# A cross-attention and FFN kernel on one core: waits reordered in all stages, and the first normalisation applied on ACT

## The reference

```python
q = X @ Wq.T + bq;  k = ctx @ Wk.T + bk;  v = ctx @ Wv.T + bv
scores = einsum('bgrqd,bgkd->bgrqk', q, k) / sqrt(16)   # masked, causal if given
out = softmax(scores) @ v;  x = x + out @ Wo.T + bo
# FFN on layernorm(x): bitlinear158 = rms_norm, 8-bit activations, ternary weights
h = layer_norm(gelu(silu(bitlinear158(x, w1, b1))), ln_g, ln_b)   # 2048 wide
x = x + bitlinear158(h, w2, b2)
```

## Time and profile before

| | us |
|---|---|
| median of 3 runs | 621.9 |
| lowest, highest | 619.96, 622.6 |
| the profiled execution | 622.59 |
| its span in the trace | 620.8 |
| PE busy | 524.9 (85%) |
| DVE busy | 489.0 (79%) |
| ACT busy | 350.8 (57%) |
| POOL busy | 135.0 (22%) |
| mean granted clock of PE | 0.926 |

### The profile page before, as it was taken

One profiled execution on the slowest core, in us unless ns is written; L12 is line 12 of the kernel. 1 busy time (PEld: TensorE's weight loads), 2 busy tenths in 40 slices (PEclk: granted clock), 3 DMA queues, 4 the chain that ended last, 5 costly groups with the idle time before them and its releaser, 6 DMA issues.

```text
span 620.8 us, 8914 instructions
## 1 busy us (share of the span) xinstructions
PE 524.9 (85%) x3374; PEld 289.5 (47%) x3374; DVE 489.0 (79%) x728; ACT 350.8 (57%) x424; POOL 135.0 (22%) x101
## 2 busy tenths in 40 slices
PE   4778497689889999999999999999869969698446
PEld 4666133362456355645564556455425523343222
DVE  3769939349699978997899789988896887648784
ACT  0244280517584867486748674867187739287630
POOL 5030031100611061106110611301140113103220
PEclk9989598797989999999999999999969989799688
DMA  8588637934422641365136412642134221100000
GB/s 315 152 234 324 211 84 191 386 116 146 86 67 105 183 99 36 125 195 114 36 124 191 102 54 76 191 98 74 40 86 102 74 75 17 38 0 1 34 34 35
DMA packets 32994, 72.17 MB, mean 116 GB/s; under 512 B 7167, under 2 KB 14529, under 8 KB 29950
## 3 DMA queue, kind: packets, MB, share of 16 engines
q1 hardware_dynamic: 31798, 71.26, 38.8%
q10 hardware_dynamic: 1152, 0.31, 0.2%
HBM read 46.50 MB, written 20.61 MB: 108 GB/s over the span
## 4 chain that ended last, share of the span: by engine, by line
PE 58%; DVE 12%; DMA 10%; ACT 9%; issue 7%; SPq 2%; POOL 1%; ACTq 1%; DVEq 0%
PE FF L853 9%; PE FF L678 7%; PE PV L792 7%; PE FF L901 6%; ACT PT L1069 5%; PE PV L775 5%; PE S L759 5%; PE S L735 5%; DVE negm L1337 4%; PE S L888 3%; PE FF L855 2%; PE PV L735 2%; DMA work<-in_w 2%; PE FF L867 2%; DMA num<-o_raw 2%
## 5 line engine op out<-in xcount | busy, mean ns | idle before, releaser
L1069 ACT ACTIVATE PT<-S 128x1024 f32<-128x1024 f32 x128 | 123.6, 1033 | 28.1 <-PE S L759 28.0
L1337 DVE TENSOR_REDUCE negm<-S 128x4 f32<-128x1024 f32 x88 | 105.6, 1215 | 24.7 <-PE S L735 23.2
L759 PE MATMUL S<-Q,K 100*128 100x512 bf16 x256 | 78.0, 413 | 27.7 <-ACT PT L1069 18.3
L775 PE MATMUL PV<-PT,vaug 128*32 128x256 f32 x1024 | 71.8, 400 | 0.4 <-ACT PT L1069 0.4
L853 PE MATMUL FF<-w1t,xqT 128*128 128x512 bf16 x256 | 67.4, 386 | 2.0 <-ACT PT L1100 1.1
L1100 ACT ACTIVATE work<-FF,s 128x512 f32<-128x512 f32 x56 | 38.5, 687 | 40.6 <-PE FF L855 40.6
L792 PE MATMUL PV<-wo_sb,num 128*128 128x512 f32 x128 | 59.9, 614 | 0.4 <-DVE negm L1337 0.4
L678 PE MATMUL FF<-xnT,wq_sb 128*128 128x256 f32 x224 | 52.8, 394 | 8.6 <-ACT xnT L1039 8.6
L735 PE MATMUL S<-K,Q 97*128 97x256 bf16 x352 | 54.5, 282 | 6.6 <-issue 3.5
L759 PEld LDWEIGHTS S<-Q,K 100*128 100x128 bf16 x256 | 18.7, 101 | 77.4 <-ACT PT L1069 54.8
L1337 DVE TENSOR_REDUCE negm<-PV 128x4 f32<-128x1024 f32 x40 | 48.8, 1221 | 6.3 <-PE PV L735 5.9
(11 more groups left out here) (196 smaller groups left out, 858.5 us busy)
## 6 DMA issues: line engine op xcount, KB each, us to landing
Q<-q_d SPq DMA_DIRECT2D x15, 768.0 KB
work<-in_w SPq DMA_DIRECT2D x8, 1024.0 KB, 11.4
q_d<-part SPq DMA_DIRECT2D x8, 768.0 KB, 3.6
x_sb<-in_x SPq DMA_DIRECT2D x8, 512.0 KB, 4.0
ctx_sb<-in_ctxT SPq DMA_DIRECT2D x8, 512.0 KB, 4.0
q_d<-part SPq DMA_DIRECT2D x8, 512.0 KB, 3.3
xb_sb<-in_x SPq DMA_DIRECT2D x8, 512.0 KB, 3.9
rec<-rec_d SPq DMA_DIRECT2D x30, 128.0 KB, 2.6
```

What stands on the lines that cost most here:

```text
L759: last = pe.matmul(where, K[0:ROWS_2, g, kt * P:(kt + 1) * P], Q[0:ROWS_2, g, 2 * pair:2 * pair + 2, :], start=not masked, stop=True)
L775: last = pe.matmul(PV[32 * r:32 * r + 32, g % 4, :], vaug[:, c % 2, kt, g, :], PT[:, n % PT_SLOTS, r, :], start=(kt == 0), stop=(kt == TT ...
L1069: act.activation(PT[:, n % PT_SLOTS, :, :], ST[n % 2][:], ACT.Exp, scale=0.25).then_inc(S["pt_made"], 1)
L1337: dve.tensor_reduce(negm[:, t, R * g:R * g + R], RING_1[n % 3][:], AX.X, ALU.max, negate=True).then_inc(S["max_made"], 1)
```

## The change

The change has seven parts.

1. The first normalisation from batch 2 on is applied on ACT as one Identity activation per half, with rs as scale and -mean * rs as bias (norm_1_apply), behind silu and before gelu; DVE adds -mean, POOL the small product (norm_1_bias). POOL's mean_3 becomes a small activation behind each gelu.
2. On PE a stage begins with project_out(f, 0), turn_max, turn_x(w), project_out(f, 1), project_q(w), project_k(a); project_v(a) comes behind the first two scores_2. ACT has keys(a) before the exps and values_in(a) behind the second. project_k keeps the wait on the reads of project_q's banks. The weight sum of w2 stands at the head of c = 1 and uses S1.
3. q_d holds four blocks: the first part once. It is read back by one transfer that repeats it three times, and a second transfer brings the other three blocks; so the first part's write is 256 KB, not 768 KB.
4. On SP the w1 chunks 0 and 1 are no longer first; load_x(2) stands behind rows_back_first; rows_back(a, 1) stands before denominators(c, 3) and numerators(c, 1); the w2 chunks are issued by POOL, their bias rows stay on SP.
5. The bias of the keys has its own semaphore, so keys(0) no longer waits for bq and bv; at the start turn_x(0) stands between project_k(0) and project_v(0).
6. On DVE key_rests(0) goes before masks, maximum(0, 0) before key_rests(1); w2's total, scale and first two passes stand early in c = 1, and the first two of w1 go on as before.
7. In c = 6 the second squares of t moves behind exp 1; in c = 7 both squares stand between exps. In the last stages turn_hq uses S0 and S1 (turn_hq_last, turn_2_last), layer_1 is not interleaved, and maximum_2 and shift come earlier.

```diff
-Q_TERMS = [slice(0, 3), slice(3, 6, 2), slice(4, 5)]
+Q_BLOCKS = [slice(0, 1), slice(1, 4, 2), slice(2, 3)]
+Q_SHARED = 3
...
-        q_d = nc.dram_tensor("q_d", (B, ROWS_SPLIT, G, R * T), BF16, kind="Internal").ap()
+        q_d = nc.dram_tensor("q_d", (B, 4 * HD, G, R * T), BF16, kind="Internal").ap()
...
+            def query_rows(a, gs, landed):
+                shared = q_d[a][0:HD, gs, :].rearrange("d g n -> d (g n)")
+                sp.dma_start(Q[0:Q_SHARED * HD, gs, :, :].rearrange("d g r t -> d (g r t)"),
+                             shared.unsqueeze(0).broadcast_to([Q_SHARED] + list(shared.shape))).then_inc(landed, 16)
+                sp.dma_start(Q[Q_SHARED * HD:ROWS_SPLIT, gs, :, :].rearrange("d g r t -> d (g r t)"),
+                             q_d[a][HD:4 * HD, gs, :].rearrange("d g n -> d (g n)")).then_inc(landed, 16)
...
+                    load_x(1)
                     load_context(1)
-                    load_x(1)
                     key_parts(0)
-                    load_x(2)
+                    weight_chunk(w1, 0)
                     query_parts(0)
                     negatives()
                     rows_back_first()
-                    weight_chunk(w1, 2)
-                    weight_chunk(w1, 3)
+                    load_x(2)
+                    for n in range(1, 4):
+                        weight_chunk(w1, n)
...
-                    denominators(c, 3)
-                    numerators(c, 1)
                 if a is not None:
                     rows_back(a, 1)
                 if c is not None:
+                    denominators(c, 3)
+                    numerators(c, 1)
+                if c is not None:
                     reciprocals(c)
                 if at_start(c):
-                    second_weights()
+                    layer_rows()
...
+            def norm_1_bias(a):
                 pool.wait_ge(S["ln1_rs"], a + 1)
-                for t in range(TT):
-                    pool.tensor_scalar(x_sb[:, t, :], x_sb[:, t, :], mv1[:, t, 0:1], rs1[:, t, 1:2],
-                                       ALU.subtract, ALU.mult).then_inc(S["xn_made"], 1)
+                tt(rs1[:, :, 3], rs1[:, :, 2], rs1[:, :, 1], ALU.mult, "ln1_bias")
+
+            def second_weights():
+                pool.wait_ge(S["w1_done"], 1)
+                for n in range(4):
+                    cols = slice(2048 * n, 2048 * n + 2048)
+                    pool.dma_start(work[:, cols], w2[:, cols]).then_inc(S[f"w2_chunk{n}"], 16)
...
             def body_of(c, a, f, t, masked):
                 w = next_front(a) if c != 0 else None
-                if w is not None:
-                    turn_x(w)
                 if f is not None:
                     project_out(f, 0, c)
                 if c is not None:
                     turn_max(c)
+                if at_start(c) or at_start(f):
+                    weight_sum(c)
+                if w is not None:
+                    turn_x(w)
+                if f is not None:
+                    project_out(f, 1, c)
                 if w is not None:
                     project_q(w)
-                if f is not None:
-                    project_out(f, 1, c)
                 if a is not None and a > 1:
-                    project_kv(a)
-                if at_start(c) or at_start(f):
-                    weight_sum(c, a)
+                    project_k(a)
                 for g in range(G + 1):
                     if c is not None and g < G:
                         scores_2(c, 2 * g, masked)
                         scores_2(c, 2 * g + 1, masked)
+                    if g == 0 and a is not None and a > 1:
+                        project_v(a)
...
-                        turn_hq(t, n, f)
+                        turn_hq_last(t, n)
...
+            def norm_1_apply(a):
+                act.wait_ge(S["ln1_bias"], a - 1)
+                for t in range(TT):
+                    act.activation(x_sb[:, t, :], x_sb[:, t, :], ACT.Identity, scale=rs1[:, t, 1:2],
+                                   bias=rs1[:, t, 3:4]).then_inc(S["xn_made"], 1)
...
-                if t is not None and a is not None:
+                if t is not None and w is not None:
                     squares(t, 1)
                 if c is not None:
 
                     act.activation(table_call[:, 1:2], table_call[:, 0:1], ACT.Exp)
                 if a is not None and a > 1:
-                    keys_and_values(a)
+                    keys(a)
                 if c is not None:
                     for n in range(16):
                         exps(c, n)
+                        if n == 1 and w is None and t is not None:
+                            squares(t, 1)
+                        if n == 1 and a is not None and a > 1:
+                            values_in(a)
...
+                    norm_1_apply(3)
                     weight_abs_sum(1)
                 if f is not None:
                     for n in range(8):
                         silu(f, n)
+                    if w is not None and w + 1 < B:
+                        norm_1_apply(w + 1)
...
+                maximum_2(t, 0)
                 residual_2(t - 1, 1)
-                maximum_2(t, 0)
...
+                shift(t, 0)
                 spread_last(t, 1)
-                shift(t, 0)
...
+                    key_rests(0)
                     masks()
-                    key_rests(0)
                     norm_1(1)
                     norm_1_apply(1)
                     query_rests(0)
                     key_masks()
                     norm_1(2)
                     query_rests(1)
+                    maximum(0, 0)
                     key_rests(1)
-                    for n in range(16):
+                    for n in range(1, 16):
...
+                    weight_total(c)
                 if c is not None:
                     max_rows(c)
+                if at_start(c) or at_start(f):
+                    weight_scale(c)
...
+                if at_start(f):
+                    quantise_weight(1, w2t[:].rearrange("p k n -> p (k n)"))
```

More of the change, by code:

```diff
@@ L393, in weights_and_biases, with layer_rows @@
                     sp.dma_start(b1_rows[n:n + 1, :], b1_d[cb:cb + 1, :]).then_inc(S["k_b1r"], 16)
-            def second_weights():
-                sp.wait_ge(S["w1_done"], 1)
-                for n in range(4):
-                    weight_chunk(w2, n)
+            def layer_rows():
                 for to, of in ((b2_bc, b2), (g_bc, ln_g), (b_bc, ln_b)):
@@ L698, in project_kv, with project_v @@
                 for k in range(KD):
-                    pe.matmul(to[:, 0:T], wkv_sb[:, k, 0:P], ctx_sb[:, k, :],
-                              start=(k == 0), stop=(k == KD - 1))
+                    last = pe.matmul(to[:, 0:T], wkv_sb[:, k, 0:P], ctx_sb[:, k, :],
+                                     start=(k == 0), stop=(k == KD - 1))
+                last.then_inc(S["k_ps"], 1)
+            def project_v(a):
+                if a == 1:
+                    pe.wait_ge(S["v_placed"], 1)
+                to = pair_of(a)
                 for t in range(TT):
@@ L751, in scores_2 @@
                     pe.wait_ge(S["m_in"], 16 * c + 16)
+                if n == 1 and c == 1:
+                    pe.wait_ge(S["w_mean"], 4)
                 if n >= 2:
@@ L973, in last_body_of @@
                     turn_xq_last(f)
[L974 to L975 removed]
+                    for n in range(8):
+                        layer_1(f, n, None)
                     layer_2_last(t - 1, 1)
[L977 to L978 removed]
                     for n in range(4):
@@ L1011, in batches @@
                 over_batches(body)
-            project_kv(0)
+            project_k(0)
             turn_x(0)
+            project_v(0)
             project_q(0)
@@ L1018, in _ @@
             project_q(1)
-            project_kv(1)
+            project_k(1)
+            project_v(1)
             pe.wait_ge(S["k_flagi"], 1)
@@ L1169, in body @@
                 if at_start(a):
-                    keys_and_values(0)
-                    for b in range(2):
-                        turned_x(b)
-                        queries(b, 0)
-                        queries(b, 1)
-                    keys_and_values(1)
-                    weight_abs_sum(0, range(2))
+                    keys(0)
+                    turned_x(0)
+                    values_in(0)
+                    queries(0, 0)
+                    queries(0, 1)
+                    turned_x(1)
+                    queries(1, 0)
+                    queries(1, 1)
+                    keys(1)
+                    values_in(1)
+                    norm_1_apply(2)
                     turned_x(2)
-                    weight_abs_sum(0, range(2, 4))
+                    weight_abs_sum(0)
                     return
```

128 lines of the change are left out of this document (56 added, 72 removed).

## The result

The changed kernel takes 677.1 us (673.3 to 682.6, 4 runs), the kernel before 621.0 (620.0 to 622.6, the three runs above and a fourth). The ratio is 1.091, 95% interval 1.081 to 1.101: slower, by some 56 us. The forecast was 624.4, with a range of 609 to 640. The profiled execution was 673.5, its span 671.6.

What follows compares the result with a forecast made beforehand. PE works almost without pause in steady stages, so gains must come from the ends. Terms +11.7 +7.8 -10.7 +2 +1 -2.4 -5.2 -1.7 = +2.5 on 622.6, less 0.7 for the median: 624.4 us, range 609 to 640.

Steps and rivals of the forecast that it cites:

- the denominators behind the rows: Stages c = 1 to 6: denominators queue behind the second half of the rows; stall 0 to 0.3 a stage, +1 in all.
- the first scores behind x(2): Start: load_x(2) stands behind all row transfers, x(2) lands at 47.8, last maximum of batch 0 ends at 73.6: +11.7.
- the price of a piece: Shared Q rows: 8 KB on one engine costs 0.34 us, bounds 0.32 and 0.49; half of Q takes 7.0 us.
- the queue ahead of the rows: Later stages: a half of the rows, 20.5 pieces, was taken to need 7.0 us, the two halves following one another.
- the zero for PE's new order: Steady stages: project_k waits 1.4 us more, but ACT's longer chain starts exp at the same time, so gain zero.
- three engines have less company: Shared Q rows: the reason for taking 0.34 us a piece, near the wide w1 loads, rather than 0.49.
- point of decision, 0.37: Steady stages: from about 0.37 us a piece the second half ends after 355.5 and rival B holds.
- rival B: At 0.49 a piece, late denominators stall DVE's reciprocal 3 to 6 a stage; start +18, c = 0 +12; 655; chance 0.13.
- c = 0: Stage of batch 0: w2 shares engines with batch 1's rows, +5.4, and the reciprocal waits for denominators; sum +7.8.
- Rival A: Shared Q rows: the repeated transfer runs on 16 engines, not 3, with Q rows of 4 us; chance 0.22.
- c = 1: Stage of batch 1: w2 summed earlier, exp 21.4 after the maximum, minus 8.8, and a loop shorter by 1.9: -10.7.
- the cover of 3.7: Steady stages: ACT's last deviations end 3.7 us before DVE uses them, so ACT's added normalisation work costs 0.

Runs made afterwards that it cites:

- v1_three: The changed kernel with the shared Q block read by three transfers of 16 rows instead of one repeating transfer: 628.9 us, ratio 1.010.
- v14_after_w2_sp: The changed kernel with w2 issued by SP behind the reciprocals of c = 0, three engines kept: 671.1 us, ratio 1.071.
- v6_three_load2_den: v5_three_load2 with denominators(3) and numerators(1) also back ahead of the second half of the rows: 617.4 us, ratio 0.991.
- v5_three_load2: v1_three with load_x(2) back ahead of the q_d transfers: 621.2 us, ratio 1.001.
- v7_w2_on_sp: v6_three_load2_den with w2 issued by SP behind the reciprocals of c = 0, as before the change: 611.9 us, ratio 0.985.
- v11_pe_order: v7_w2_on_sp with PE's old order, turn_x at the stage head and project_q ahead of the second project_out: 601.8 us, ratio 0.968.
- v12_w2_late: v7_w2_on_sp with sum, scale and first two passes of w2 in their old places in c = 1: 618.2 us, ratio 0.996.
- v9_pool_norm: v7_w2_on_sp with the first normalisation from batch 2 on applied by POOL again, not ACT: 612.9 us, ratio 0.984.

## Why the prediction was wrong

The mechanism that decides was in it, and in the forecast's own case: three engines, the denominators behind the rows, the first scores behind x(2). Three steps failed: the price of a piece, the queue ahead of the rows, and the zero for PE's new order.

**The shared rows: the price of a piece, and what is ahead in the queue.** The prediction took 0.34 us for 8 KB on one engine, near the wide loads. At the start, 45 pieces from about 30.4 (28.85, when the first Q transfer was issued, and 1.5) to the landing of x(2) at 53.9 are 0.52 each, over its upper bound of 0.49. (The rows went out 2.1 earlier than the forecast's 31, which hid part of this.) Two windows of the changed kernel, then two of v1_three at about the same place:

```profile
40.00:44.00 4.00, 0.00 (x0) 0.00 (x0) 0.00 (x0) 0.00 (x0) 0.00 (x0) 0.50 1.03 253
44.00:48.00 4.00, 0.00 (x0) 0.00 (x0) 0.00 (x0) 0.00 (x0) 0.00 (x0) 0.50 1.06 244
```

```profile
44.00:46.00 2.00, 0.00 (x0) 0.00 (x0) 1.29 (x2) 0.00 (x0) 0.00 (x0) 0.50 0.98 403
46.00:48.00 2.00, 0.00 (x0) 0.00 (x0) 1.96 (x9) 0.40 (x1) 0.89 (x2) 0.50 1.04 434
```

In both the w1 chunks run at this time with all engines busy. In v1_three the rows are over and the engines move over 400 GB/s; in the changed kernel three engines still read q_d, and all 16 together move 250. So the argument "three engines have less company" was wrong twice. The other engines are not idle here, they go on to the loads that wait behind, and all move little while q_d rows are being read, as in the earlier trace rows (0.55 MB in 2 us, 275 GB/s). And where they are nearly idle, in the window of c = 3 above, a piece still costs 0.50. This makes +18.3 of the start where +11.7 stood. Within the later stages the second error adds to it: the sum let the rows of a half begin when they were issued. In c = 3 the first Q transfer went out at 313.25 and PE was released only near 329, 14.3 us from 1.5 behind the issue, for 20.5 pieces. By 0.52 a piece these are 10.7. For the other 3.6 stand the context, the residual and the key parts (1.4 MB), issued in the 7 us ahead of it; that these make them up is argued from the queue and was not tried. The prediction counted none of these for batches after the first. Its point of decision, 0.37, was passed, and rival B's mechanism was at work: +18 of steady cost in c = 3 to 5, where the forecast had +1 and B 3.5 a stage.

**c = 0.** +7.8 was forecast, bound +12; it was +23.4. Its two waits are there, both mis-sized: PE's first scores of batch 1 waited 12.1 (forecast 5.4), the reciprocal 10.7 (forecast 4.2). Some 3 more are in the ruler: m_d went out 6.6 behind the end of the last maximum, before 3.8. v1_three with 16 engines has still +14.6, v14_after_w2_sp with three engines and no w2 +12.9: each of the two, w2 beside the rows or the three engines, gives more than half without the other. The new order on SP has its part too: with it undone as well, c = 0 loses another 7 (66.2 to 58.9, v6_three_load2_den).

**Start, x(2).** Right as a mechanism: norm_1(2) waits for x(2), and v5_three_load2 gives back 8.2 with this one move. Rival A's x(2) at 43.5 was 44.7 in v1_three. The piece "25.8 from x(2) to the last maximum" was 26.3 (53.9 to 80.2).

**c = 1.** exp began 22.2 after the start of the last maximum (149.88 to 172.03) where 21.4 was forecast and 30.2 was before:

```profile
172.03 1.94 ACT L1083 ACTIVATE PT<-S 128x1024 f32<-128x1024 f32 x2
```

So the gain ahead of exp was there, 8.0 for 8.8. The loop behind it grew by 5.0 (53.5 from the first exp to the next m_d, 48.6 before), where the forecast had it shorter by 1.9. By the ruler, which starts at the late m_d, the stage gained 6.0 for 10.7. v1_three, with 16 engines, has -10.5. The reason was not the one given: the forecast gave the gain to w2's early arrival and to project_q's release. With w2 12 us later (v7_w2_on_sp) and with turn_x at the head again (v11_pe_order) c = 1 stays at 60.9 and 59.9. The place of the weight sum, scale and first passes carries 7 of the 13 between 73.8 and 60.9 (v12_w2_late, 68.1); part of this 7 may be arrival, since the last sum ended 1.8 behind m_d in that trace and 2.0 ahead of it in v7_w2_on_sp. What carries the other 6 stays open.

**Steady stages.** The forecast's zero for the PE order is the step that failed by its argument: it compared only when exp begins, and took 1.4 us of PE's waiting for nothing because ACT's chain was longer. But PE is the bound of a steady stage, and the window of c = 4 of the kernel before would have said so (PE busy 60.26 of 62.80):

```profile
315.40:378.20 62.80, 60.26 (x422) 34.25 (x421) 55.90 (x86) 41.80 (x51) 16.24 (x12) 1.00 0.39 108
```

It does not catch up between the exps; a wait of 1.93 where 1.04 was is paid. The half of the edit that seems to help, project_v among the exps, was counted as zero too: with the old order beside it (v11_pe_order) a stage falls from 62.8 to 61.2. Before, PE waited for ACT's first exps in c = 4, 0.89 and then 0.31:

```profile
330.71 0.61 PE L759 MATMUL S<-Q,K 100*128 100x512 bf16 x2 [0.89 <-ACT PT L1069]
```

In v11_pe_order, with project_v at this place, these two waits are gone. project_v was not moved alone, so that it brings the 1.6 is argued from these 1.2. The two halves cancelled to +0.5 in v1_three (mean of 63.3, 62.4 and 64.1), so that the total hid the error.

**ACT for POOL.** Right: the cost is nothing that the runs can tell (v9_pool_norm), as the cover of 3.7 said.

**c = 2, c = 6, c = 7 and the tail.** c = 2 was +2.5 for +2 in the changed kernel, though v1_three, without the three engines, has +0.5, so this agreement is chance. In c = 6 exp began 6.5 behind m_d where 12.1 was, as forecast (6.8):

```profile
504.42 1.93 ACT L1083 ACTIVATE PT<-S 128x1024 f32<-128x1024 f32 x2
```

With 16 engines c = 6 gained 2.6 (v1_three), forecast 2.4; in the changed kernel the rows took this back, and it is 1.3 longer. From m_d of c = 7 to the end it was -6.8, forecast -6.9, but made up otherwise. turn_hq lost its wait of 5.40, and inside layer_1 a new one came, for ACT's silu, which stands behind ACT's issue of four transfers (4.25) and a table load (1.28):

```profile
595.89 1.89 PE L855 MATMUL FF<-w1t,xqT 128*128 128x512 bf16 x4 [4.20 <-ACT work L1114]
```

so project_out(7) ended 3.3 earlier behind m_d where 5.2 was forecast, and the tail gained 3.5 where 1.7 was. That the sum came out is chance.

**The chances.** 0.41 on slower was the largest of the three; the range was too narrow. It ended at 640, though rival B, at 655, stood on bounds read from the rows. B had the right mechanism and still falls 18 short of the 50.8 measured: 11.4 of this in c = 0 and 4.7 in c = 1. The price had a row of its own for just this traffic, 0.49, and the forecast went by the other row, for a reason that no row supported.

## What to carry to other kernels

Before a transfer gets a repeated or split dimension, look at what its slowest dimension leaves for the engines: here a 3 put a third of the transfer on each of 3, and everything queued behind on these waited, down to 8 KB that took 27 us. The same bytes as three transfers of 16 rows cost two issues more each time and gave back 48 us. Where an engine is the bound of a stage, sum its waits and not only the start of the next engine's work; and size a queue by all that stands ahead of the transfer in it.

## What the runs showed of the hardware

- A transfer with 3 on its slowest dimension ran on about 3 of 16 engines (share 0.18), one with 4 at a share of 0.21 in a slice, 3.4 of 16, with the edges of the slice in it.
- While the rows of q_d are read, all transfers together move some 250 GB/s with every engine busy (253 and 244 with the rows on 3 engines, 275 with them on 16), and in v1_three over 400 (403 and 434) once these are over. Why the others are slow then was not tried and stays open.
- A piece of 8 KB of these rows costs its engine 0.50 us even when 13 of 16 engines are nearly idle (share 0.18, 47 GB/s), and 0.49 with all busy; a piece of w1 costs 0.32.
- A wait of 1.93 us on PE was in one stage followed by a granted clock of 0.50 for some 3 us; in the next, with the same wait, the clock stayed at 1.00. The stages were 64.1 and 62.4 long.
- The changed kernel scatters more (673 to 683) than the kernel before (619 to 625 over all its runs) or v11_pe_order (601.0 to 602.8).
